# A two-layer graph network kernel on one core: six ring slots in place of four, longer runs of equal matmuls on TensorE, one accumulator

## What is computed

```python
h = relu(layernorm(x))
u = tanh([h, t] @ W1 + b1) @ W2 + b2
XB = h @ B.T
x = x + u + adj @ XB - sum(adj, axis=1) * XB            # first layer
h = relu(layernorm(x))
feats = h @ W                                           # 8 heads of 8
scores = leaky_relu(a_self[i] + a_neigh[j]) - 1e10 * (1 - adj[i, j])
x = x + relu(softmax(scores) @ feats + bias)            # second layer
```

## Time and profile before

| | |
|---|---|
| median of 3 runs (lowest to highest) | 904.38 us (903.35 to 905.34) |
| the profiled execution, its time | 904.73 us |
| its span, first to last instruction | 903.5 us |
| TensorE matmuls / weight loads busy | 776.9 us (86%) / 266.7 us (30%) |
| VectorE / ScalarE / POOL busy | 729.3 us (81%) / 128.5 us (14%) / 173.4 us (19%) |
| granted TensorE clock, mean | 0.941 of 2.4 GHz |
| read from HBM | 277.10 MB, 311 GB/s over the span; about 280 and 425 GB/s by turns in the page's slices |
| marks | chunk 0's first matmul at 14.2 us, strip 1 from 79 us, last strip's matmuls end at 795 us, then the tail |

### The profile page before, as it was taken

How to read it: one execution, slowest core, us unless ns; L and a number is a source line. 1 busy time by engine, 2 the same in 40 slices (tenths; PEclk the granted TensorE clock), 3 DMA queues, 4 the chain that set the end, 5 groups by cost and what they waited for, 6 DMA issues and landing times.

```text
span 903.5 us, 13331 instructions
## 1 busy us (share of the span) xinstructions
PE 776.9 (86%) x5222; PEld 266.7 (30%) x5222; DVE 729.3 (81%) x958; ACT 128.5 (14%) x212; POOL 173.4 (19%) x160
## 2 busy tenths in 40 slices
PE   3898999999999999999999999999999999940000
PEld 1333232333333333333332323233333333320000
DVE  5889968989898989898989898998989897952111
ACT  2424011111111111111010201111111111110000
POOL 1000302020110202020202020202011020217774
PEclk9999999999999999999999999999999999985555
DMA  9797879697979797979798897979797979502221
GB/s 375 280 428 288 321 291 422 271 424 288 425 288 426 284 429 280 429 291 418 319 390 364 345 410 300 420 290 422 289 421 287 425 283 429 214 11 40 60 49 41
DMA packets 37267, 281.58 MB, mean 312 GB/s; under 512 B 14336, under 2 KB 18560, under 8 KB 20736
## 3 DMA queue, kind: packets, MB, share of 16 engines
q1 hardware_dynamic: 33152, 277.12, 74.9%
q0 software_dynamic: 4096, 4.20, 2.0%
HBM read 277.10 MB, written 4.19 MB: 311 GB/s over the span
## 4 chain that ended last, share of the span: by engine, by line
PE 74%; POOL 7%; DVE 5%; issue 4%; DMA 4%; SPq 4%; ACT 0%; POOLq 0%; DVEq 0%
PE acc L726 44%; PE row_sums L734 22%; POOL gathered L367 7%; DMA ring<-in_adj_t 4%; SPq L255 4%; DVE max_hi L514 2%; PE ps_hid L754 2%; PE ps_feat L796 1%; PE ps_xb L775 1%; PE ps_acc L768 1%; PE ps_turn L782 1%; PE ps_acc L771 1%; PE ps_acc L773 1%; PE ps_turn L789 1%; DVE max_lo L513 0%
## 5 line engine op out<-in xcount | busy, mean ns | idle before, releaser
L726 PE MATMUL acc<-ring,x_pb 128*64 128x512 f32 x2048 | 462.8, 601 | 18.4 <-DMA ring<-in_adj_t 18.4
L513 DVE TENSOR_TENSOR max_lo<-max_lo,ring 128x2048 f32<-128x2048 f32 x96 | 220.6, 2298 | 44.7 <-DMA ring<-in_adj_t 44.2
L734 PE MATMUL row_sums<-ring,ones_cols 128*32 128x512 f32 x2048 | 240.0, 597 | 0.0
L726 PEld LDWEIGHTS acc<-ring,x_pb 128*64 128x64 f32 x2048 | 141.0, 138 | 326.1 <-issue 326.1
L514 DVE TENSOR_TENSOR max_hi<-max_hi,ring 128x2048 f32<-128x2048 f32 x96 | 219.7, 2289 | 0.0
L358 POOL DMA_INDIRECT cand<-in_adj,cls_row x64 | 78.0, 1218 | 663.5 <-DVE cls_row L543 648.9
L734 PEld LDWEIGHTS row_sums<-ring,ones_cols 128*32 128x32 f32 x2048 | 56.5, 109 | 151.6 <-issue 149.8
L367 POOL DMA_INDIRECT gathered<-feats_dram,best x64 | 62.8, 981 | 19.5 <-issue 19.5
L651 DVE TENSOR_TENSOR gathered<-gathered,bias_row 128x512 f32<-128x512 f32 x8 | 5.6, 703 | 67.5 <-DMA gathered<-feats_dram,best 67.5
L508 DVE TENSOR_TENSOR max_lo<-ring 128x2048 f32<-128x2048 f32 x16 | 36.7, 2292 | 4.4 <-DMA ring<-in_adj_t 2.5
L510 DVE TENSOR_TENSOR max_hi<-ring 128x2048 f32<-128x2048 f32 x16 | 36.6, 2288 | 4.2 <-DMA ring<-in_adj_t 3.9
(11 more groups left out here) (95 smaller groups left out, 423.3 us busy)
## 6 DMA issues: line engine op xcount, KB each, us to landing
ring<-in_adj_t SPq DMA_DIRECT2D x128, 2048.0 KB, 11.3
x_tq<-in_x SPq DMA_DIRECT2D x1, 2048.0 KB, 30.8
feats_dram<-feats SPq DMA_DIRECT2D x16, 128.0 KB, 2.3
out<-gathered SPq DMA_DIRECT2D x8, 256.0 KB
x_pb<-in_x SPq DMA_DIRECT2D x1, 1536.0 KB, 7.8
cand<-in_adj,cls_row POOLq DMA_INDIRECT x64
gathered<-feats_dram,best POOLq DMA_INDIRECT x64
x_pb<-in_x SPq DMA_DIRECT2D x1, 512.0 KB, 4.6
```

The costliest lines, as they stand in the source:

```text
L513: dve.tensor_tensor(max_lo[:, :], max_lo[:, :], lo, ALU.max).then_inc(lo_done, 1)
L726: last = pe.matmul(acc[parity][at:at + D, :], x_pb[:, c * CB + b, :], slot(c)[:, b * W:(b + 1) * W], start=(c == 0 and b < 2), stop=(c == ...
L734: last = pe.matmul(row_sums[at:at + QUAD, :], ones_cols[:, :], slot(c)[:, b * W:(b + 1) * W], start=(c == 0 and b < 4), stop=(c == NC - 1 ...
```

## The change

- RING is 6. Strips 1 to 15 run in 5 laps of LAP = 3 (24 chunks, a multiple of 6, so that slot and count are constants in the code); `at_slot` and `landed` give them.
- To make room, `gathered` is a view of the ring's slot 0; the gathers therefore also wait for the last `runmax`. `h_t` has two blocks of x one above the other in its partitions and is half as long. The general code uses the ring.
- `turn_first` turns two blocks at a time (4 transposes of [128, 128]), by turns into one of two banks; `place` and `strip_h` are one copy each in place of two.
- TensorE's order in a strip is written out: sums 0, 1; `turn_maxima`, `turn_sums`; products 0 to 3; sums 2 to 5, `turn_h1`; products 4 to 7; sums 6, 7; `features`, `mlp_hidden`. The whole strip starts with a wait for `rows_copied`.
- There is one accumulator bank. `acc_full` tells ScalarE that the strip's products are done; the copy of `acc` waits for it, the copy of `row_sums` for all of the strip.
- In strip 0 the sums of a chunk don't wait for the normalised x.
- The feats store is issued by ScalarE, behind a wait for its own copy, and no longer by SP.

The diff, cut to its core:

```diff
-RING = 4
+RING = 6
+LAP = 3
+NR = (S - 1) // LAP
...
-        gathered = sb("gathered", [P, NB, D])
+        gathered = ring[:, 0:NB * D].rearrange("p (t d) -> p t d", d=D)
...
-        h_t = sb("h_t", [P, N])
+        h_t = sb("h_t", [P, N // 2])
...
+        def at_slot(u, c):
+            return (u * NC + c) % RING
+
+        def landed(r, u, c):
+            return r * (16 * LAP * NC // RING) + 16 * ((u * NC + c) // RING + 1)
...
-            with sp.Fori(1, S) as s:
-                for c in range(NC):
-                    load(s, c)
-                store_feats(s - 1)
-            store_feats(S - 1)
+            with sp.Fori(0, NR) as r:
+                for u in range(1, LAP + 1):
+                    for c in range(NC):
+                        load(r, u, c)
...
             pool.wait_ge(feat_stored, 16 * S)
+            pool.wait_ge(runmax_done, S)
...
-                for half, src in enumerate(pro_banks):
-                    act.copy(h_by_block[:, g * (CB // TB) + half], src).then_inc(pro_h, 1)
+                act.copy(h_by_pair[:, 2 * g:2 * g + 2], pro_banks[g % 2].rearrange("d (f m p) -> d f m p", f=2, m=2))\
+                    .then_inc(pro_h, 1)
...
-            def finish_strip(s, parity, last=False):
-
+            def finish_strip(s, last=False):
+
+                act.wait_ge(acc_full, s + 1)
+                act.copy(acc_sb[:, :], acc[0][:, :]).then_inc(acc_copied, 1)
                 act.wait_ge(pe_chunk, s * NC + NC)
-                act.copy(acc_sb[:, :], acc[parity][:, :]).then_inc(acc_copied, 1)
                 act.copy(row_sb[:, :], row_sums[:, :]).then_inc(rows_copied, 1)
...
                 act.copy(feats[:, bass.ds(s * (TB * FA), TB * FA)],
                          ps_feat[:, :, :].rearrange("q t f -> q (t f)")).then_inc(feat_done, 1)
-
+                act.wait_ge(feat_done, s + 1)
+                dst = feats_by_q[:, bass.ds(s, 1), :].rearrange("q a (k d) -> q (a k) d", d=D)
+                act.dma_start(dst, feats_v[:, bass.ds(s * TB, TB), 0:D]).then_inc(feat_stored, 16)
...
+            with act.Fori(0, NR) as r:
+                for u in range(LAP):
+                    finish_strip(strip_at(r, u))
+                    tanh(strip_at(r, u + 1))
+            finish_strip(S - 1, last=True)
...
-                for k in range(CB):
-                    last = pe.transpose(pro_banks[k // 4][:, k % 4, :], x_pb[:, g * CB + k, :], ident[:, :])
+                if g >= 2:
+                    pe.wait_ge(pro_h, g - 1)
+                for j in range(CB // 2):
+                    pair = x_pb[:, g * CB + 2 * j:g * CB + 2 * j + 2, :].rearrange("p b d -> p (b d)")
+                    last = pe.transpose(pro_banks[g % 2][:, j * P:(j + 1) * P], pair, ident[:, :])
...
+            def strip(r, u):
+
+                prev = strip_at(r, u - 1)
+                pe.wait_ge(rows_copied, strip_at(r, u))
+                for c in (0, 1):
+                    arrived(r, u, c)
+                    sums(u, c)
+                turn_maxima(prev)
+                turn_sums(prev)
+                for c in (0, 1):
+                    products(u, c).then_inc(pe_chunk, 1)
+                for c in (2, 3):
+                    arrived(r, u, c)
+                    products(u, c)
+                for c in (2, 3):
+                    sums(u, c).then_inc(pe_chunk, 1)
+                for c in (4, 5):
+                    arrived(r, u, c)
+                    sums(u, c)
+                turn_h1(prev, ps_turn)
+                for c in (4, 5):
+                    products(u, c).then_inc(pe_chunk, 1)
+                for c in (6, 7):
+                    arrived(r, u, c)
+                    last = products(u, c)
+                last.then_inc(acc_full, 1)
+                for c in (6, 7):
+                    sums(u, c).then_inc(pe_chunk, 1)
+                features(prev)
+                mlp_hidden(strip_at(r, u))
```

More of the change, by code:

```diff
@@ L154, in build @@
         pe_chunk = sem("pe_chunk")
+        acc_full = sem("acc_full")
         lo_done = sem("lo_done")
@@ L294, in _ @@
                 sp.wait_ge(gen_copied, NB // 4)
-                sp.dma_start(neigh_dram, h_t[0:HEADS, :]).then_inc(gen_neigh_stored, 16)
+                sp.dma_start(neigh_dram, ring[0:HEADS, 2 * N:3 * N]).then_inc(gen_neigh_stored, 16)
                 sp.wait_ge(gen_neigh_stored, 16)
@@ L412, in strip_h @@
             def strip_h(s):
-                for k in range(2):
-                    act.copy(h_strip[k * D:(k + 1) * D, :].rearrange("d (m q) -> d m q", q=P),
-                             h_by_k[:, 2 * k:2 * k + 2, bass.ds(s * P, P)]).then_inc(strip_h_done, 1)
-            def finish_strip(s, parity, last=False):
+                act.copy(h_strip[:, :].rearrange("d (m q) -> d m q", q=P), h_by_m[:, :, bass.ds(s * P, P)])\
+                    .then_inc(strip_h_done, 1)
+            def finish_strip(s, last=False):
+                act.wait_ge(acc_full, s + 1)
+                act.copy(acc_sb[:, :], acc[0][:, :]).then_inc(acc_copied, 1)
                 act.wait_ge(pe_chunk, s * NC + NC)
-                act.copy(acc_sb[:, :], acc[parity][:, :]).then_inc(acc_copied, 1)
                 act.copy(row_sb[:, :], row_sums[:, :]).then_inc(rows_copied, 1)
@@ L500, in normalise, with fold_chunk @@
                                          ALU.max, ALU.mult).then_inc(pro_norm, 1)
[L502 to L506, removed]
+            def fold_chunk(r, u, c):
+                n = chunks_before(r, u) + c
+                k = at_slot(u, c)
+                dve.wait_ge(chunk_in[k], landed(r, u, c))
+                lo, hi = slot(k)[:, 0:HALF], slot(k)[:, HALF:2 * HALF]
                 if c == 0:
@@ L617, in _ @@
             constants()
-            fold_chunk(0, NC - 1)
+            fold_chunk(0, 0, NC - 1)
             fold_maxima(0)
-            with dve.Fori(1, S) as s:
-                strip(s)
+            with dve.Fori(0, NR) as r:
+                for u in range(1, LAP + 1):
+                    strip(r, u)
             residual(S - 1)
@@ L718, in turn_first, with arrived, products @@
                 last.then_inc(pro_turned, 1)
-            def products(s, c, parity):
-                pe.wait_ge(chunk_in[c % RING], s * (16 * NC // RING) + 16 * (c // RING + 1))
+            def arrived(r, u, c):
+                pe.wait_ge(chunk_in[at_slot(u, c)], landed(r, u, c))
+            def products(u, c):
                 for b in range(CB):
                     at = (b % 2) * D
-                    last = pe.matmul(acc[parity][at:at + D, :], x_pb[:, c * CB + b, :], slot(c)[:, b * W:(b + 1) * W],
+                    last = pe.matmul(acc[0][at:at + D, :], x_pb[:, c * CB + b, :], slot(at_slot(u, c))[:, b * W:(b + 1) * W],
@@ L727, in products, with sums @@
                                      start=(c == 0 and b < 2), stop=(c == NC - 1 and b >= CB - 2))
                 return last
-            def sums(c):
+            def sums(u, c):
                 for b in range(CB):
                     at = (b % 4) * QUAD
-                    last = pe.matmul(row_sums[at:at + QUAD, :], ones_cols[:, :], slot(c)[:, b * W:(b + 1) * W],
+                    last = pe.matmul(row_sums[at:at + QUAD, :], ones_cols[:, :], slot(at_slot(u, c))[:, b * W:(b + 1) * W],
@@ L735, in sums @@
                                      start=(c == 0 and b < 4), stop=(c == NC - 1 and b >= CB - 4))
                 return last
[L738 to L749, removed]
@@ L751, in mlp_hidden @@
             def mlp_hidden(s):
-                pe.wait_ge(strip_h_done, 2 * s + 2)
+                pe.wait_ge(strip_h_done, s + 1)
                 for k in range(2):
-                    last = pe.matmul(ps_hid[:, k * (W // 2):(k + 1) * (W // 2)], w1_sb[:, k * HID:(k + 1) * HID],
-                                     h_strip[:, :], start=True, stop=True)
+                    last = pe.matmul(ps_hid[:, :].rearrange("c (m k q) -> c k m q", m=2, k=2)[:, k],
+                                     w1_sb[:, k * HID:(k + 1) * HID], h_strip[:, :],
+                                     start=True, stop=True)
@@ L774, in turn_sums @@
                 for m in range(2):
-                    last = pe.matmul(ps_xb[:, :, :].rearrange("q (h m) d -> q m h d", m=2)[:, m],
+                    last = pe.matmul(ps_xb[:, 2 * m:2 * m + 2, :].rearrange("q k d -> q (k d)"),
                                      h_strip[:, m * P:(m + 1) * P], b_t_diag[:, :], start=True, stop=True)
@@ L798, in features, with strip @@
                 last.then_inc(feat_ready, 1)
[L800 to L811, removed]
+            def strip(r, u):
+                prev = strip_at(r, u - 1)
+                pe.wait_ge(rows_copied, strip_at(r, u))
[25 more added lines that the diff above has]
+                mlp_hidden(strip_at(r, u))
+            pe.wait_ge(pool_const, 3)
             for c in range(NC):
+                arrived(0, 0, c)
+                if c < NC - 1:
+                    sums(0, c)
                 pe.wait_ge(pro_norm, c + 1)
```

(9 more changed lines are left out.)

63 lines of the change are left out of this document (29 added, 34 removed).

## The result

The changed kernel takes **970.56 us** (median of 4 runs, 970.40 to 971.58) against 904.52 us: the ratio is 1.073, 95% interval 1.072 to 1.075. Forecast were 949 us and a range of 932 to 968. The direction and the wait for ScalarE were right, the share of the clock was too small, and the time lies 2.6 us outside the range.

What follows compares the result with a forecast made beforehand. TensorE was taken to bound strips 1 to 15. Span 903.5 - 15.0 (seams) + 55.5 (wait for ScalarE) + 8.0 (clock) - 4 (prologue) = 948, plus 1.2: 949 us; range 932 to 968.

Steps and rivals of the forecast that it cites:

- The bound and the price of the seams: Strips 1 to 15: TensorE bounds; a seam costs 0.13 or 0.14 us; longer runs gain 0.82 us a strip.
- no idle time inside them: Strips 1 to 15 before the change: TensorE busy all 47.52 us of a strip.
- The wait for ScalarE: Strip starts: TensorE idles 3.7 us until ScalarE's list ends with the row_sums copy, 15 times, +55.5 us.
- the store's 0.9: ScalarE at strip starts: waiting for its own feats copy and issuing the store adds 0.9 us to the stall.
- The clock: Strip starts: 5 of 15 go slow on TensorE at 1.6 us each, +8.0 us (0 to 24).
- rival (a): Strip starts: every one goes slow, +24 us of low clock, 965 us in all; chance 0.20.
- the prologue: Before the first mark: cheaper turn_first and fewer h copies, a 3.8 us idle ahead of chunk 6; net -4 us.
- the tail: Behind the last turn_sums: the 106 us there stay.
- The range: Whole kernel: 932 to 968 us, the high end being the all-slow case with 0.2 us more stall.
- Parts at nothing: VectorE, six slots, feats store off SP, tail gathers, POOL's wait: no effect; TensorE meets no DMA wait.

Runs made afterwards that it cites:

- e3_store_later: The changed kernel with the feats-copy wait and feats store behind the next row_sums copy, ScalarE's loop cut to two strips a turn: 954.25 us, ratio 1.054.
- e10: The changed kernel with nothing but TensorE's loop of five laps written out: 970.43 us, ratio 1.074 to the kernel before.
- e1: The changed kernel with ScalarE's copies of the next strip's acc and row_sums ahead of the feats copy, store and tanh: 897.36 us, ratio 0.992.
- e7: e1 with TensorE's loop of five laps written out, same instructions in the same order: 888.57 us, ratio 0.984 to the kernel before.
- e4_filler: The changed kernel with 8 matmuls of unread result between mlp_hidden and the wait for rows_copied: 958.98 us, ratio 1.060.
- e12: e4_filler with TensorE's loop written out and 4 filler matmuls in place of 8: 941.34 us, ratio 1.042 to the kernel before.
- e8_best: e7 with the small weights asked for behind the second chunk and strip 0's copies ahead of tanh(0): 881.11 us, ratio 0.975.
- e5: e1 with a ring of four slots and a loop body of one strip on every engine: 891.73 us, ratio 0.987.

## Why the prediction was off

- **The bound and the price of the seams** were right: 46.70 us a strip worked out, 46.7 measured without the wait. Only "no idle time inside them" was not quite so: two of the strips before held an idle of 1.15 and 1.02 us, and one of 1.34 stood behind the last strip; the sum between the marks, 711.9, has them in it.
- **The wait for ScalarE** was right in place, releaser, parts and size: 3.7 us forecast, 3.56 to 3.72 measured; feats copy, issue, table load (1.28, with nothing further between it and tanh) and the two copies follow each other as listed; the store's 0.9 was 0.87. Over the 15 waits, the last counted with the `turn_maxima` in it, 54.4 against 55.5 us.
- **The clock is the step that failed**: "I take one strip start in three, 5 of 15, to go slow". All went slow, and one start costs 2.0 us on the mean and not 1.6: 28.7 us and not 8.0. These 20.7 are nearly all of the 20.9 by which the span was missed; the wait, 1.1 less, the prologue, 1.6 more, and the tail, 0.3 less, about cancel. Two things were wrong in the step. I read how far into an idle the clock fell (2.9, 4.1 and 4.8 us) and assumed that an idle which ends sooner escapes. But the fall can come after work has resumed: at 392.4 in the changed kernel (0.35 us behind) and at 440.06 in e3_store_later (1.2 us behind). The lengths of the idles themselves, 4.28, 2.97 and 5.07, all followed by slow work, were the better guide, and they said what rival (a) says. And the price came from one idle, where 16 products had paid 1.6. In the changed kernel the starts pay 1.5, 1.7 and 2.9 by turns (first sums 5.09, 5.34 and 6.49 against 3.64); the one with 6.49 stayed at the low clock from 337.8 to 344.6, 6.8 us, and the other two for 3.4 (443.6 to 447.0, 392.4 to 395.8). Rival (a) at 965, with a chance of 0.20, had the mechanism; with 28.7 in place of 24 it is 970.
- **The range** reached 968 and missed since its upper end took rival (a) at the single price of 1.6.
- **The prologue** gained 2.4 and not 4. The order of events was right: SP held in its first weight load for 33.51 us, the weights done at 48.6, chunk 6 at 56.9 us. TensorE had wanted it at 51.8, a microsecond sooner than I had it, so the idle there was 5.13 and not 3.8.
- **Parts at nothing** held: no DMA wait of TensorE after the prologue, the tail is unchanged. That the feats store off SP gains nothing was not taken by itself in any run. The fetch of the longer loop body I had overlooked; in the changed kernel it costs nothing (e10), in a kernel without the wait about 7 us (e1 to e7, by their ratios), of which 6.0 are idles in the trace.

## What to carry to other kernels

When small steps are moved on one engine, write down the program order of the engine that serves them: a copy that frees a bank is as late as the last thing listed ahead of it, here a tanh with its table load. If the matmul engine gets a wait at each turn of a loop, charge it the low clock behind every one that is as long as the shortest idle seen to cost it, and look for its price in several places. That is caution and no rule: in e4_filler two such idles cost nothing. And compare the number of instructions in a loop's body with the instruction queue of the page before making the body longer.

## What the runs showed of the hardware

- TensorE's clock: between strips of dense matmuls, 14 idles of 1.69 to 1.85 us never lowered it (e12, clock 1.00 over 500 us), and idles of 2.6 to 3.7 us did at every start in two kernels (e3, changed kernel). The fall came from 2.6 us into the idle to 1.2 us after its end.
- The length of an idle alone does not decide. In e4_filler idles of 2.70 and 2.99 us, behind the filler, left the clock at 1.00, and those of 3.38 and 3.72 lowered it. Ahead of the last `turn_sums`, an idle of 2.19 us left it at 1.00 until all the small matmuls behind it were done (e1, e7), while one of 2.26 us was followed by a fall 1.4 us after its end (e3). And in the prologue of e8_best an idle of 1.64 us with a microsecond of small transposes ahead of it and `mlp_hidden(0)` behind it was followed by slow sums (5.34). What else it hangs on stays open.
- How long the clock then stays low varies between starts of the same kernel, 3.4 us at two of three and 6.8 at the third (changed kernel), in a pattern of three with the loop written out as well (e10), so the loop is not its cause. What sets it stays open.
- Going back to the start of a TensorE loop of 1950 records cost 1.1 to 2.2 us in e1 and 2.9 to 3.7 us in e4, whose body was longer; with 1300 records (the kernel before) or 650 (e5) no idle was seen there.
